# A two-layer pipeline on one core: scores by 64 keys, TensorE's rounds in a loop, another order in the last pair

## What is computed

```python
xn = layernorm(x)
x = x + rwkv6_attention(xn) * silu(sparse_ffn(xn))   # layer 0; hidden kept 2 of 4 by magnitude
xn = layernorm(x)
x = x + ssd_attention(xn) * silu(gated_ffn(xn))      # layer 1
```

```python
L = where(tri, exp(cs[..., :, None] - cs[..., None, :]), 0)      # decay from key j to query i, j <= i
scores = einsum('znid,znjd->znij', Cc, Bc) * L
y_within = einsum('znij,znjh->znih', scores, Xc)
states = einsum('znj,znjd,znjh->zndh', exp(cs[..., -1:] - cs), Bc, Xc)
y_across = einsum('znid,zndh,zni->znih', Cc, S_prev, exp(cs))
```

## Time and profile before

| | us |
|---|---|
| median of 3 runs | 716.09 |
| the profiled execution, whole | 717.52 |
| its span | 715.7 |
| PE busy in it | 702.5 |
| DVE busy | 496.1 |
| ACT busy | 338.1 |
| POOL busy | 76.7 |

### The profile page before, as it was taken

How to read it: one execution, slowest core, us unless ns; L and a number is a source line. 1 busy time by engine, 2 the same in 40 slices (tenths; PEclk the granted TensorE clock), 3 DMA queues, 4 the chain that set the end, 5 groups by cost and what they waited for, 6 DMA issues and landing times.

```text
span 715.7 us, 18156 instructions
## 1 busy us (share of the span) xinstructions
PE 702.5 (98%) x7010; PEld 597.9 (84%) x7010; DVE 496.1 (69%) x1214; ACT 338.1 (47%) x671; POOL 76.7 (11%) x85
## 2 busy tenths in 40 slices
PE   7999999999999999999999999999999999999998
PEld 5777788888888788887888878888788888888887
DVE  5995988528884488755896568954789529895133
ACT  1423782147711586206852068421783237821790
POOL 6301011101110011100111001110011100110020
PEclk9999999999999999999999999999999999999999
DMA  7911460125501364012720236202370025601370
GB/s 231 408 44 30 136 103 18 22 82 143 96 2 30 102 128 83 16 30 89 149 61 16 52 120 110 47 15 74 104 128 23 16 77 136 105 12 25 122 120 16
DMA packets 139572, 59.46 MB, mean 83 GB/s; under 512 B 119728, under 2 KB 131312, under 8 KB 137968
## 3 DMA queue, kind: packets, MB, share of 16 engines
q1 hardware_dynamic: 139504, 58.44, 33.9%
HBM read 44.18 MB, written 14.24 MB: 82 GB/s over the span
## 4 chain that ended last, share of the span: by engine, by line
PE 87%; DVE 5%; issue 3%; DMA 2%; ACT 2%; SPq 1%; POOL 0%; DVEq 0%; POOLq 0%; ACTq 0%
PE psum L1542 68%; PE psum L1651 2%; PE psum L1763 2%; PE psum L1778 2%; ACT BC L626 1%; PE psum L1596 1%; PE psum L1621 1%; PE psum L1816 1%; PE psum L2002 1%; PE psum L1684 1%; PE psum L1863 1%; PE psum L1633 1%; PE psum L1789 1%; PE psum L1735 1%; PE psum L1724 1%
## 5 line engine op out<-in xcount | busy, mean ns | idle before, releaser
L626 ACT ACTIVATE BC<-psum 64x256 f32<-64x256 f32 x128 | 81.6, 637 | 1.9 <-PE psum L1542 0.2
L1542 PE MATMUL psum<-xn1T,sb_n_gate 128*128 128x256 f32 x256 | 61.3, 382 | 0.0
L1542 PE MATMUL psum<-xn1T,sb_n_up 128*128 128x256 f32 x256 | 60.5, 379 | 0.0
L1542 PE MATMUL psum<-xnT,sb_f_gate 128*128 128x256 f32 x240 | 57.8, 383 | 0.0
L1542 PE MATMUL psum<-xnT,sb_f_up 128*128 128x256 f32 x240 | 57.0, 379 | 0.0
L1542 PEld LDWEIGHTS psum<-xn1T,sb_n_gate 128*128 128x128 f32 x256 | 48.0, 190 | 6.8
L1542 PEld LDWEIGHTS psum<-xn1T,sb_n_up 128*128 128x128 f32 x256 | 48.2, 190 | 6.3
L757 ACT ACTIVATE thFB<-psum 128x512 f32<-128x512 f32 x8 | 4.8, 597 | 102.1 <-PE psum L1542 102.1
L1542 PEld LDWEIGHTS psum<-xnT,sb_f_up 128*128 128x128 f32 x240 | 45.2, 189 | 6.8 <-issue 0.3
L1542 PEld LDWEIGHTS psum<-xnT,sb_f_gate 128*128 128x128 f32 x240 | 44.7, 189 | 7.2 <-DVE xnT L1205 0.2
L1542 PE MATMUL psum<-sb_n_down,hidB 128*128 128x256 f32 x224 | 49.5, 379 | 0.0
(11 more groups left out here) (265 smaller groups left out, 1494.4 us busy)
## 6 DMA issues: line engine op xcount, KB each, us to landing
cs_row<-cs_dram SPq DMA_DIRECT2D x8, 1024.0 KB, 5.0
x_dram<-gate SPq DMA_DIRECT2D x8, 512.0 KB, 2.8
cs_half<-cs_dram SPq DMA_DIRECT2D x16, 256.0 KB, 5.8
hidB<-x_dram SPq DMA_DIRECT2D x8, 512.0 KB, 5.7
b_dram<-B_turned SPq DMA_DIRECT2D x32, 128.0 KB, 3.5
hidB<-b_dram SPq DMA_DIRECT2D x8, 512.0 KB, 4.2
X<-in_x SPq DMA_DIRECT2D x9, 256.0 KB, 2.9
XT<-in_x_turned SPq DMA_DIRECT2D x8, 256.0 KB, 2.9
```

Source lines behind the costliest of these rows:

```text
L626: ins = a_.activation(cols[:, par, 2 * pair:2 * pair + 2, :], src[64 * par:64 * par + 64, :, s, :], ACT.Identity)
L1542: ins = t_.matmul(ps(t, name)[first_row:first_row + rows, col:col + n], w, x, start=(k == 0), stop=(k == len(ws) - 1))
```

## The change

- `KEY_ROWS`: in the second 128 of every two chunks the keys are laid out with their two halves of 64 exchanged. So `cs_pos`, `Xrow` and `Brow` are loaded by three transfers each rather than one (even chunks whole, odd chunks in two halves), with the same bytes, and the waits count accordingly. POOL's select becomes three: even chunks, odd chunks, and the exchanged half again with another base.
- `ssd_scores`: a chunk's product by 128 keys becomes two by 64 keys: the first 64 keys with all 128 queries, the last 64 keys with the last 64 queries, on 64*64 tiles. The zero quarter is not computed; what stands in the bank there is masked. A `sem_inc` stands behind each `open_bank`.
- PE is written by `rounds(pe, one)` as the others are: six pairs are a loop. The 23 pads go. Waits for weights that only the first pair needs stand in every iteration.
- The last pair, written out by itself, has other orders on ACT, DVE and PE.
- DVE: `end_args` moves behind `level_next(a, 5)`; in its old place a wait for the store of the output of the round before.
- First round: `kept_busy` with 19 rather than 39 products.

```diff
+KEY_ROWS = [(slice(0, P), 0, slice(0, P)), (slice(0, 64), 1, slice(64, P)), (slice(64, P), 1, slice(0, 64))]
...
-                    sp_.dma_start(cs_pos[:, :], cs_dram.rearrange("(c p) -> p c", p=P),
-                                  allow_slow_non_contiguous=True).then_inc(cs_loaded, 16)
+                    pos = cs_dram.rearrange("(c two p) -> p c two", two=2, p=P)
+                    by_two = cs_pos[:, :].rearrange("p (c two) -> p c two", two=2)
+                    for to, r, from_ in KEY_ROWS:
+                        sp_.dma_start(by_two[to, :, r], pos[from_, :, r], allow_slow_non_contiguous=True).then_inc(cs_loaded, 16)
...
-                    sp_.dma_start(Brow.rearrange("p q c d -> p (q c) d"),
-                                  b_dram.rearrange("(c p d) -> p c d", p=P, d=SD)).then_inc(B_rows, 16)
+                    keys = b_dram.rearrange("(c two p d) -> p c two d", two=2, p=P, d=SD)
+                    for to, r, from_ in KEY_ROWS:
+                        sp_.dma_start(Brow.rearrange("p q (c two) d -> p (q c) two d", two=2)[to, :, r, :],
+                                      keys[from_, :, r, :]).then_inc(B_rows, 16)
...
-                    g.affine_select(out=cs_row[:, :, :], in_=cs_row[:, :, :], compare_op=ALU.is_ge, fill=NEG, base=0,
-                                    pattern=[[0, NQ * SCH], [1, P]], channel_multiplier=-1).then_inc(cs_masked, 1)
+                    by_two = cs_row[:, :, :].rearrange("p (c two) q -> p c two q", two=2)
+                    for last, r, two, base in ((P, slice(0, P), 0, 0), (P, slice(0, P), 1, 64), (64, slice(0, 64), 1, -64)):
+                        m = by_two[r, :, two, :]
+                        ins = g.affine_select(out=m, in_=m, compare_op=ALU.is_ge, fill=NEG, base=base,
+                                              pattern=[[0, NQ * SCH // 2], [1, P]], channel_multiplier=-1)
+                        if last == P:
+                            did(ins)
+                    ins.then_inc(cs_masked, 1)
...
-                    ffn_tanh_0()
-                    out_scaled()
-                    ffn_tanh(b, "n2", thB[0], None, "n0")
+                    if a.reg is not None:
+                        ffn_tanh_0()
+                        out_scaled()
+                        ffn_tanh(b, "n2", thB[0], None, "n0")
+                    else:
+                        ffn_tanh(b, "n2", thB[0], None, "n0")
+                        out_scaled()
+                        ffn_tanh_0()
...
-                    end_args()
+
+                    dve.wait_ge(out_stored, b.count(16, 16))
+                    dve.sem_inc(passed, 1)
                     level_next(a, 4)
                     level_next(a, 5)
+                    end_args()
...
-                    hidden_n(b, 2)
-                    residual_0()
-                    hidden_n(b, 3)
-                    normed_1()
+                    if a.reg is not None:
+                        hidden_n(b, 2)
+                        residual_0()
+                        hidden_n(b, 3)
+                        normed_1()
+                    else:
+                        residual_0()
+                        hidden_n(b, 2)
+                        normed_1()
+                        hidden_n(b, 3)
...
                 for name in names:
                     open_bank(t, name)
+                    pe.sem_inc(passed, 1)
...
-                    for s in range(NQ):
-                        r = half_rows(s)
-                        ins[s] = t_.matmul(ps(t, names[s])[:, i * P:(i + 1) * P], Bf[r, c * P:(c + 1) * P],
-                                           Cf[r, c * P:(c + 1) * P], start=True, stop=True)
+                    for first in range(2):
+
+                        k, at = slice(c * P + 64 * first, c * P + 64 * first + 64), 64 * (first ^ (c % 2))
+                        for s in range(NQ):
+                            r = half_rows(s)
+                            ins[s] = t_.matmul(ps(t, names[s])[at:at + 64, i * P + 64 * first:(i + 1) * P], Bf[r, k],
+                                               Cf[r, c * P + 64 * first:(c + 1) * P], start=True, stop=True)
...
-                first_a, first_b = not b, a and b and b.off == 0
+                first_a, first_b = not b, a and b and (a.reg is not None)
...
-                    if a.off < NT - 1:
+                    if a.reg is not None:
...
+                        out_0()
                         up_n(b, 2)
-                        out_0()
                         gate_n(b, 3)
                     up_n(b, 3)
-
-                    for _ in range(23):
-                        pe.sem_inc(passed, 1)
...
-                    kept_busy(["mix_w", "mix_k"], 39)
+                    kept_busy(["mix_w", "mix_k"], 19)
...
-            one(Tile(None, 0, first=True), None)
-            for n in range(1, NT):
-                one(Tile(None, n), Tile(None, n - 1))
-            one(None, Tile(None, NT - 1, last=True))
+            rounds(pe, one)
```

22 lines of the change are left out of this document (12 added, 10 removed).

## The result

The changed kernel takes 720.7 us (median of 6 runs), the kernel before in the same comparison 716.37 us. Five of the six runs lie between 719.11 and 721.41 us, with a median of 720.22; the sixth, a slow one of 1307.87 us, is left out of the ratio. The ratio is 1.0051, 95% interval 1.0035 to 1.0066: slower by about 3.7 us. The forecast was 714.5, just faster, with a range of 711 to 720. Slower had a chance of 0.25, under the second rival.

The account below looks back on a forecast made before the run. PE, 98% busy, was taken to bound the kernel, with DVE pacing the stretch around the scores. Scores -1.05, loop +0.6, last pair -0.7 and first round -0.4 sum to -1.55 us: 716.09 becomes 714.5, range 711 to 720.

Parts of the forecast that it names:

- second rival: PE's back edge and block ends in small-tile stretches: instruction transfers show, 719.9 us with 1 us per iteration; chance 0.25.
- What bounds the kernel: PE, busy 98% of the span, bounds the whole; around the scores the stretch moves at DVE's pace.
- scores: ssd_scores on 64*64 tiles: 0.56 us saved on PE, 0.15 us per pair surviving DVE's queue, -1.05 us in all.
- PE's loop: Six iterations on PE: register arithmetic and a branch add 0.1 us each, +0.6 us; removed pads cost nothing before.
- Instruction transfers: I take no change: PE's loop: 57 blocks in all, only 0.2 us of PE idle in a round, so transfers hidden, no change.
- ACT, DVE and POOL branch back without a stop: Argument against rival 2's costly back edge on PE: the other engines' rows show no stop at their branches.
- Keys by 64 through memory: Six more transfers per pair on SP's queue delay nobody: cost 0, ends 0 and 0.2 us per pair.
- Last pair: New orders remove PE's waits for mixed_w and xn1T: -0.7 us, ends 0 and -0.92.
- First round: Half the filling passes let L1816 start at 11.2 us: -0.4 us, ends 0 and -0.6.
- Tail: More issues ahead of B's rows against faster scores: taken as 0, ends -0.5 and +1.1 us.
- POOL and end_args: Three selects finish about 180.2 rather than 178.94; moved end_args fits DVE's 0.40 us wait before L1210: cost 0.

Follow-up runs that it names:

- one transfer: Changed kernel with one transfer each for cs_pos, Xrow and Brow and one select on POOL, keys not exchanged: 718.98 us, ratio 1.0021.
- ends: Kernel before with only the last pair's order on ACT, DVE and PE and 19 rather than 39 filling products: 715.17 us, ratio 0.9979.
- experiment 2: Kernel before with PE's rounds in a loop, the 23 pads away and the first pair's waits in every iteration: 721.02 us, ratio 1.006.
- experiment 5: Kernel before without its 23 pads, nothing else: 717.77 us, ratio 1.0018.
- experiment 12: Kernel before with a loop of 8 iterations of one sem_inc on PE in the first round: 718.75 us, one execution, only its trace read.
- experiment 13: Kernel before with PE's rounds in a loop, pads away, and 128 sem_inc spread over the first round: 732.32 us, ratio 1.0209.
- experiment 7: Kernel before with cs_pos, Xrow and Brow loaded by three transfers each, keys not exchanged: 722.07 us, ratio 1.0073.
- experiment 9: Kernel before with 25 sem_inc spread over the first round's dense stretches, to provoke a block transfer meeting k's load: 717.75 us, ratio 1.0012.
- experiment 10: Kernel before with three transfers each for cs_pos, Xrow and Brow, not exchanged, and 128 sem_inc in the first round: 721.72 us, ratio 1.0066.
- experiment 1: Changed kernel with PE's rounds written out one behind the other again instead of the loop: 721.02 us, ratio 1.0067.
- experiment 14: Kernel before with PE's rounds in a loop, pads away, and 160 sem_inc in the first round: 721.81 us, ratio 1.0073.
- experiment 4: Changed kernel with two rounds in each iteration of PE's loop, 2 taken branches rather than 5: 727.25 us, ratio 1.0144.

## Why the prediction was wrong, step by step

*What bounds the kernel* and *scores*: right as far as they went. DVE's queue did hold the stretch up to the second product with the decays, and of PE's saving of 0.33 us at the next L1571 (forecast 0.56) there were 0.20 left at L1811 (forecast 0.15). In the changed kernel the wait for k took it back. No run has the faster scores alone. By subtraction, scores = (one transfer 1.0021) - (loop 1.006) + (1 - ends 0.9979) = -0.0018, or -1.3 us with an uncertainty of about 1.5, which can't be told from nothing; the forecast was -1.05.

*PE's loop*: the step that failed. Forecast +0.6 us, measured +4.3 us: 3.0 for the loop and 1.3 for the pads' removal (experiments 2 and 5). The arithmetic was about 0.2 us per iteration, where 0.1 was taken. The two other items were named in the prediction and then counted at nothing. "Instruction transfers: I take no change" left out that a far branch is a transfer with the stream standing still, 3.6 to 4.0 us, about as long as the issued work lasts (3.8 us); its visible part was 0.1 to 0.5 us in five iterations. And block ends moved among the small tiles: up to 0.9 us in some iterations. The prediction saw the removed pads only as 3.6 us of covered stream. What they did was done by their number: they made the round 7 x 256 instructions, so that ends stayed where they hurt little. The count, 1792 in every middle pair of the trace before, was to be had. Rival 2 named the place, the back edge, and priced a block at 2.0 us by a store's landing; its threshold of 0.6 us per iteration was met, at 0.7. That its sum with 1 us per iteration, 719.9, comes near the 720.7 is luck: it counted six branches where five are taken, gave the stops inside the round no price of their own, and some 2 us came from the split transfers, which were put at nothing. The sentence that ACT, DVE and POOL branch back without a stop was no evidence for PE, whose loop is 1876 instructions long. The Trainium skill, in "Runtime: NRT & Kernel Launch", section Instruction fetch mechanics, says that a taken branch whose target is out of the window forces a fetch; experiments 2, 12 and 13 agree with that, at 3.8 us against 0.21.

*Keys by 64 through memory*: forecast 0 with an end of 0.2 us per pair, measured about 2.1 us in the changed kernel and 5.2 us alone in the kernel before. The step asked who waits for Brow. It did compute that two more issues end before the k stores at 187.50, but it took the issue's own 0.38 us; three take 1.69 us of the queue, since there are 0.28 us between issues. And it did not follow the queue to its last member. k landed at 196.0 and PE came to it at 196.44 in the trace before, a cover of 0.4 us; the first pair there already waited for it. Most of the 5.2 us are not the issues: 4.3 us are waits for five loads of k that a block's transfer met (experiments 7, 9 and 10), which the prediction had no term for.

*Last pair*: right when alone, -0.7 forecast, -0.5 to -0.9 measured; in the changed kernel the wait for k and a block end ate it. *First round*: right, -0.4 forecast, -0.5 measured. *Tail*: right, near zero (49.2 us before, 49.0 after, 48.8 to 49.8 in all traces). *POOL and end_args*: right; DVE's stretch is not later.

The parts in ratios are 1.006 (loop), 0.9979 (ends), 0.9982 (scores) and 1.0030 (transfers). That they come to 1.0051, the result, proves nothing: the last two were formed as differences, so that the sum has to. And parts don't add up strictly here, since each edit moves the block ends, as experiments 1 and 10 show.

What stays open: what fills the 1.3 us before and the 1.4 us after the transfer within a far branch; what decides the moment at which the next block is fetched, and with it whether a block end stops PE; and what the faster scores are worth alone.

## What to carry to other kernels

On an engine whose program is long, treat the instruction stream as a queue with a supply of its own: count the instructions of a round modulo 256, find the block transfers in the trace, and see which small-tile stretches and which late loads they meet, before adding or removing even a no-op. A loop over a long body paid its far branch every time here; it would be free only if the work already issued outlasted it, and its first instruction should stand at the start of a block (experiments 13 and 14). When transfers are added to a queue, follow the queue to its last member and check that one's cover.

## What the runs showed of the hardware that was not expected

- A taken branch on PE took 3.6 to 4.0 us where the target was 1809 or 1876 instructions back (experiments 2 and 14, changed kernel), and 0.21 to 0.24 us where it was three instructions back (experiment 12); not taken it took 0.08 us.
- After such a branch the block behind the target's comes late: with 27 instructions left in the first block, PE stood for 1.4 to 1.9 us (experiment 13).
- PE's stops for instructions lie at block ends, 256 instructions apart, but most block ends cause none. A stop of 0.4 us and more ended 1.2 to 1.65 us after the end of a block's transfer.
- A block's transfer (mostly 0.9 to 1.4 us) that met a load of 256 KB early moved its landing from 2.7 to between 3.2 and 4.2 us after the issue; met late, it was harmless in 25 of 28 cases, and moved it to 4.2 to 4.7 us in three.
- DVE's product of 128x448, 0.62 us, took 2.8 us when it started while POOL ran a product of 128x1024 of 2.38 us; one that was already under way kept its 0.62 us (experiment 4, three times each).
